# Matmuls that only keep TensorE running, an opening in another order, and keys and values projected two batches ahead, in a decoder layer on one core

## What is computed

```
x = x + self_attention(layernorm(x))          # 2 heads of 64, rotary, causal
x = x + cross_attention(layernorm(x), ctx)    # 16 heads of 8, 1601 keys
x = x + ffn(layernorm(x))                     # 512 hidden, exact gelu, weights changed per batch

Q = split_heads(query @ Wq + bq); K = split_heads(ctx @ Wk + bk); V = split_heads(ctx @ Wv + bv)
attn = softmax(einsum("bhqd,bhkd->bhqk", Q, K) / sqrt(8)); out = attn @ V @ Wo + bo
```

## Time and profile before

| | |
|---|---|
| three timed runs | 414.47, 417.73, 417.07 us; median 417.07 |
| the profiled execution | 413.62 us |
| its span | 411.8 us |
| busy, share of the span | TensorE 87%, VectorE 74%, ScalarE 73%, GpSimd 32% |
| mean granted TensorE clock | 0.925 |
| first maximum, first score | 39.3 us, 60.2 us |
| end of unit 0, of batch 0, 1, 2, 3 | 90.8, 150.0, 236.7, 323.2, 391.9 us |

### The profile page before, as it was taken

How to read it: one execution, slowest core, us unless ns; L and a number is a source line. 1 busy time by engine, 2 the same in 40 slices (tenths; PEclk the granted TensorE clock), 3 DMA queues, 4 the chain that set the end, 5 groups by cost and what they waited for, 6 DMA issues and landing times.

```text
span 411.8 us, 11548 instructions
## 1 busy us (share of the span) xinstructions
PE 357.9 (87%) x4598; PEld 164.8 (40%) x4598; DVE 306.6 (74%) x692; ACT 299.4 (73%) x637; POOL 131.6 (32%) x205
## 2 busy tenths in 40 slices
PE   1645988989989989999898999998989999798946
PEld 0332333444534444444344444444334344353334
DVE  2373998779889988798788887998778899690022
ACT  1321226888979799889697898897697998969921
POOL 5721000379120206897200137992000036000010
PEclk9966555999999999999999999999899999999968
DMA  7063370003507312235160331343211420000000
GB/s 294 12 240 122 139 249 40 2 27 130 173 27 169 123 38 60 93 130 163 35 173 14 107 96 53 121 136 96 80 40 47 130 61 21 2 15 2 2 0 15
DMA packets 22203, 35.77 MB, mean 87 GB/s; under 512 B 1604, under 2 KB 19694, under 8 KB 22150
## 3 DMA queue, kind: packets, MB, share of 16 engines
q1 hardware_dynamic: 22150, 35.05, 26.8%
HBM read 19.25 MB, written 11.96 MB: 76 GB/s over the span
## 4 chain that ended last, share of the span: by engine, by line
PE 47%; DMA 13%; POOL 12%; ACT 11%; DVE 7%; issue 5%; SPq 4%; POOLq 0%; ACTq 0%; DVEq 0%
PE wsum L1013 16%; PE score L1027 10%; PE ring L983 8%; PE ring L1047 8%; DMA q_rows<-q_parts 5%; ACT probs L873 5%; POOL k_parts L547 4%; DMA k_rows<-k_parts 4%; POOL k_rest L584 3%; POOL k_parts L589 3%; DVE part_max L690 2%; DMA k_unit<-k_rows 2%; DMA q_unit<-consts 1%; SPq L435 1%; POOL xn L600 1%
## 5 line engine op out<-in xcount | busy, mean ns | idle before, releaser
L690 DVE TENSOR_REDUCE part_max<-ring 128x1 f32<-128x401 f32 x512 | 261.0, 568 | 43.8 <-PE ring L1047 42.8
L873 ACT ACTIVATE probs<-score 128x512 f32<-128x512 f32 (+1 forms) x416 | 223.1, 597 | 41.6 <-PE score L1027 38.1
L1047 PE MATMUL ring<-k_unit,q_unit 51*128 51x401 bf16 x512 | 143.2, 355 | 9.9 <-DMA q_unit<-consts 5.1
L1013 PE MATMUL wsum<-probs,v_unit 128*32 128x256 f32 (+1 forms) x1664 | 135.7, 394 | 2.0 <-ACT unit_ctx L878 2.0
L1027 PE MATMUL score<-q_unit,k_unit 51*128 51x256 bf16 (+1 forms) x832 | 123.9, 278 | 7.3 <-ACT probs L873 5.0
L1027 PEld LDWEIGHTS score<-q_unit,k_unit 51*128 51x128 bf16 (+1 forms) x832 | 47.2, 97 | 100.6 <-ACT probs L873 60.9
L1047 PEld LDWEIGHTS ring<-k_unit,q_unit 51*128 51x128 bf16 x512 | 47.3, 95 | 30.1 <-DVE part_max L690 10.8
L1013 PEld LDWEIGHTS wsum<-probs,v_unit 128*32 128x32 f32 (+1 forms) x1664 | 39.7, 109 | 41.3 <-issue 24.6
L547 POOL TENSOR_TENSOR max_parts<-neg_max,c_sb 128x8 bf16<-128x8 f32 x16 | 3.4, 210 | 150.8 <-DVE neg_max L694 150.7
L621 POOL TENSOR_SCALAR prob_norm<-prob_self,prob_rsum 128x128 f32<-128x128 f32 (+1 forms) x12 | 9.0, 766 | 43.1 <-DVE prob_rsum L766 43.1
L927 ACT ACTIVATE v_aug<-ring 128x128 f32<-128x128 f32 (+1 forms) x60 | 10.5, 261 | 16.1 <-PE ring L983 16.1
(11 more groups left out here) (111 smaller groups left out, 290.3 us busy)
## 6 DMA issues: line engine op xcount, KB each, us to landing
k_unit<-k_rows SPq DMA_DIRECT2D x32, 300.2 KB
v_unit<-v_aug SPq DMA_DIRECT2D x16, 234.0 KB, 5.9
ctx_sb<-ctx_t SPq DMA_DIRECT2D x4, 800.5 KB, 7.4
k_rows<-k_parts SPq DMA_DIRECT2D x4, 601.5 KB, 3.2
k_rows<-k_parts SPq DMA_DIRECT2D x4, 599.2 KB, 3.4
k_rows<-k_parts SPq DMA_DIRECT2D x4, 401.0 KB, 4.1
k_rows<-k_parts SPq DMA_DIRECT2D x4, 399.5 KB, 4.1
even<-ffn_rows SPq DMA_DIRECT2D x3, 512.0 KB, 3.8
```

The costliest lines, as they stand in the source:

```text
L690: v_.tensor_reduce(part_max[:, par, q, head, hp, c:c + 1], ring[s][:, 0:CW], AX.X, ALU.max)\
L873: a_.activation(probs[0:rows, i % PB, :], score[i % EB][0:rows, :], ACT.Exp)\
L1013: last = mm(wsum[32 * j:32 * j + 32, 0:S], v_unit[0:rows, u, VQ * t + VW * j:VQ * t + VW * j + 32], probs[0:rows, i % PB, S * (j // 2):S * ...
L1047: mm(ring[s][:, 0:CW], q_unit[rows, u, hp, P * q:P * (q + 1)], k_unit[rows, u, L * hp + (CW - 1) * c:L * hp + (CW - 1) * c + CW], start=Tr ...
```

## The change

Four things are changed together.

1. **Kept matmuls.** `keep(n)` issues n matmuls of a zero tile, 128 by 128 by 512, bf16, into the first bank of scores. 20 stand at the very start, before TensorE waits for weights; 21 in six other places up to unit 0; 13 in two places at the end.
2. **The opening's order.** `U0` to `U6` and the load of values move ahead of unit 0's maxima. Batch 1's keys and values (`K0` to `K3`, `V0` to `V3`) and their stores stand between these maxima. Batch 0's qk_rot goes from GpSimd to VectorE. Of batch 0's keys the 32 rows of unit 0 are stored first, with a semaphore of their own; their load follows at once, and then come the other 96 rows. GpSimd's adds x1_bo and x2_b2 wait in batch 0 and at the end until VectorE has made the normalised tile.
3. **Two batches ahead.** In `SIDE` the items of keys and values name batch b+2 instead of b+1, so batch 2 has none. ctx_sb and v_aug are there twice.
4. **The queue.** The key load of a later batch's first unit moves from `store1` to `split`, behind the store of queries.

```diff
 SIDE = {
-    (3, 0): [("ctx", 2)],
+    (3, 0): [("ctx", 3)],
...
-    (1, 8): [("prep", "q", 1), ("prep", "store1", 1)], (1, 9): [("prep", "split", 1)],
+    (1, 8): [("prep", "q", 1), ("prep", "store1", 2)], (1, 9): [("prep", "split", 1)],
...
-FIRST = [("ln1", 0), ("ln1", 1), ("xT", 0), ("qk", 0), ("qks", 0), ("K0", 0), ("K1", 0), ("e0", 0), ("e1", 0), ("soft", 0),
...
+FIRST = [("keep", 20), ("ln1", 0), ("ln1", 1), ("xT", 0), ("qk", 0), ("qks", 0), ("K0", 0), ("K1", 0), ("keep", 5),
+         ("e0", 0), ("e1", 0), ("soft", 0), ("pn", 0), ("K2", 0), ("K3", 0), ("store0", 0), ("v", 0), ("xT", 1), ("keep", 6),
+         ("qk", 1), ("pT0", 0), ("pT1", 0), ("av", 0), ("store1", 0), ("wo", 0), ("U0", 0), ("U1", 0), ("U2", 0), ("U3", 0),
+         ("keep", 3), ("ln2", 0), ("x2T", 0), ("q", 0), ("split", 0), ("qks", 1), ("keep", 3), ("pick", 0),
+         ("U4", 0), ("U5", 0), ("U6", 0), ("load", 0), ("keep", 2)]
+
+BETWEEN = (("K0",), ("K1",), ("K2",), ("K3", "store0"), ("V0",), ("V1",), ("V2",), ("V3", "store1"))
+POST_LAST = ["OT", "Wo", "keep", "ln3", "x3T", "low0", "low1", "h0", "h1", "keep", "out"]
+KEEP_LAST = (10, 3)
...
-    for i in range(7):
-        plan += [("M", 0, k) for k in range(4 * i, 4 * i + 4)] + [("prep", f"U{i}", 0)]
...
+    for i in range(MU // 4):
+        plan += [("M", 0, k) for k in range(4 * i, 4 * i + 4)] + [("prep", name, 1) for name in BETWEEN[i]]
+    plan += [("ctx", 2)]
+    return plan + [("M", 1, k) for k in range(4)] + [("keep", 2), ("mT", 0)] + [("M", 1, k) for k in range(4, AHEAD_FIRST)]
...
+                        first = 0 if b else D // UB
+                        for t0, t1 in RUNS if first else ():
+                            sp.dma_start(k_rows[b, t0:t1, 0:first, keys].rearrange("t r n -> r t n"),
+                                         k_parts[0:first, 0:t1 - t0, keys]).then_inc(first_keys_written, 16)
+                        if first and h == 1:
+                            load_keys(b, 0)
                         for t0, t1 in RUNS:
-                            sp.dma_start(k_rows[b, t0:t1, :, keys].rearrange("t r n -> r t n"),
-                                         k_parts[:, 0:t1 - t0, keys]).then_inc(keys_written, 16)
-                        if h == 1:
-                            load_keys(b, 0)
+                            sp.dma_start(k_rows[b, t0:t1, first:D, keys].rearrange("t r n -> r t n"),
+                                         k_parts[first:D, 0:t1 - t0, keys]).then_inc(keys_written, 16)
...
                         if b:
+                            load_keys(b, 0)
                             load_queries(b, 0)
...
+                        if b == 1:
+                            pool.wait_ge(first_keys_written, 32 * len(RUNS))
+                        if b:
+                            pool.wait_ge(keys_written, 32 * len(RUNS) * b)
...
+                        else:
+                            pool.wait_ge(xn2_done, 1)
...
+                    else:
+                        pool.wait_ge(xn3_done, B)
...
+                    if nb == 0:
+                        wait_drained(("prep", "qk", nb))
+                        wait_drained(item)
+                        v_.tensor_tensor(qk_rot[:, :], rope_a[:, :], rope_b[:, :], ALU.add).then_inc(qk_done, 1)
...
+                    if nb:
+                        act.wait_ge(k_split[c // 2], 4 * nb)
...
+            def keep(n):
+
+                for _ in range(n):
+                    mm(score[0][:, :], still[:, 0:P], still[:, :], start=True, stop=True)
```

More of the change, by code:

```diff
@@ L148 @@
 }
-FIRST = [("ln1", 0), ("ln1", 1), ("xT", 0), ("qk", 0), ("qks", 0), ("K0", 0), ("K1", 0), ("e0", 0), ("e1", 0), ("soft", 0),
-         ("pn", 0), ("K2", 0), ("K3", 0), ("store0", 0), ("v", 0), ("xT", 1), ("qk", 1), ("pT0", 0), ("pT1", 0), ("av", 0),
-         ("store1", 0), ("wo", 0), ("ln2", 0), ("x2T", 0), ("q", 0), ("split", 0), ("qks", 1), ("pick", 0)]
-POST_LAST = ["OT", "Wo", "ln3", "x3T", "low0", "low1", "h0", "h1", "out"]
+FIRST = [("keep", 20), ("ln1", 0), ("ln1", 1), ("xT", 0), ("qk", 0), ("qks", 0), ("K0", 0), ("K1", 0), ("keep", 5),
[6 more added lines that the diff above has]
+KEEP_LAST = (10, 3)
 AHEAD = (14, 13, 7, 10)
@@ L665, in _ @@
             v_ = nc.vector
+            v_.memset(still[:, :], 0.0).then_inc(still_set, 1)
             dve.wait_ge(x_in, 16)
@@ L1131, in prep @@
                     at = CW * int(name[1])
-                    strips(ring[s][:, 0:CW], W("Wk"), ctx_sb[:, at:at + CW]).then_inc(filled[s], 1)
+                    strips(ring[s][:, 0:CW], W("Wk"), ctx_sb[:, nb % 2, at:at + CW]).then_inc(filled[s], 1)
                 elif name == "pick":
```

72 lines of the change are left out of this document (42 added, 30 removed).

## The result

| | before | changed |
|---|---|---|
| median, same chip | 415.8 us (414.3 to 417.7) | 399.6 us (398.1 to 402.6) |
| ratio | | 0.962, 95% interval 0.954 to 0.969 |
| profiled execution | 413.6 us, span 411.8 | 398.1 us, span 396.2 |

The change makes the kernel 3.8% faster. Every ratio here is taken over the executions within 1.5% of the fastest of the same kernel; the medians are over all of them. The forecast was 392.5 us in a range of 386 to 402: the direction holds and the time lies in the range, 7 us above the point. It lies outside the 387 to 397 that the forecast gave its own case. Profile against profile the gain is 15.5 us where the sum said 22.3.

A forecast was written before the change was run, and what follows sets the result against it. TensorE was taken to bound the steady part, latency and the low clock the opening, small steps at low clock the end. Terms summed to -22.3 from 413.6, 391.3; a third of 3.4 added gave 392.5 us, range 386 to 402.

The forecast's parts named there:

- its own case: Whole kernel: the changes act as its terms say, time within 387 to 397 us; chance 0.64.
- the sum: Whole kernel: all terms from first score to end added, -22.3 us on the profiled 413.6, so 391.3.
- First 20 kept matmuls, faster first projections: Start: kept matmuls end near 7.5 us without delay; projections at full clock bring first energies at 13.4, 1.7 us earlier.
- Keys of unit 0: Opening: storing 32 rows first lands in 2.3 us, load issued at 27.9, first maximum at 36.2, -3.0 us.
- Strips between the maxima: Opening: eight rounds at VectorE's pace take 16.2 us for 17.3, -1.1; GpSimd's queue adds 0.7, the turn gives 0.3.
- The 1.3 for two rounds at the low clock: First maxima: TensorE idles some 2.5 us before them, so 1.3 us was added for two rounds at the low clock.
- Unit 0 at the full clock, -4.9: First unit after the first score: steps of 1.24 us at full clock, 8.6 us for 13.7; bounds 0 and 5.1.
- the three signs: Wrong if clock reads 0.50 in 45 to 70 us, first maximum stays at 39, or third batch stays above 82.
- Waits for queries, -5.0 and -1.6: Steady part: TensorE's three waits for q_unit, 5.1 us, vanish, and the half clock behind the third with them.
- Third batch, -5.5: Third batch: without keys and values it issues 7.46 us fewer TensorE records, ending at 77 us; bounds 0 and 7.5.
- End, -2.9: End of the kernel: kept matmuls hold the full clock and GpSimd's add waits; output at 407.0, 2.9 us sooner.
- the rival of a low clock: Opening: clock stays low through maxima and unit 0, maxima 21.9 us for 17.5, no 4.9 gain, 402 us; chance 0.15.

The follow-up runs named there:

- Experiment 6: The changed kernel with all 128 rows of the first batch's keys stored before unit 0's load, instead of 32 rows first; median 407.7 us.
- experiment 10: The changed kernel run once more, unedited; median 400.2 us, ratio 0.959, its profiled execution 405.2 us.
- experiment 8: The changed kernel with more kept matmuls, the second batch's first key strips ahead of the first maximum, and matmuls of zeros in unit 0 and Gelu passages; median 398.2 us.
- experiment 9: The changed kernel with the third batch's context load earlier, 398.2 us; also with a key strip earlier, kept matmuls and matmuls of zeros, 393.8 us; a third kernel followed.
- experiment 5: The changed kernel with keys and values projected one batch ahead and none between the first maxima; median 400.1 us, ratio 0.963.
- experiment 4: The changed kernel with 25 zero-adding matmuls of 256 columns in the last batch's Gelu passage; median 399.3 us.
- Experiment 2: The kernel before the change with only the kept matmuls added, at the nearest places; median 415.8 us, ratio 0.992.
- Experiment 1: The changed kernel with every kept matmul left out; median 405.7 us.
- 7: The changed kernel with the second batch's first two key strips ahead of the first maximum, replacing two kept matmuls, other strips spread over eight rounds; median 398.2 us.
- the last of 9: The 393.8 us kernel (early context load, key strip ahead, kept matmuls and matmuls of zeros) with 14 more kept matmuls in the opening; median 398.4 us.

## Why the prediction was right and wrong, step by step

- *First 20 kept matmuls, faster first projections.* Right: they ended at 7.4 (7.5 forecast), energies at 13.3 (13.4), VectorE's key split at 23.7 (24.0). Their records lie 0.43 us apart to 4.9 us, so the first ones ran at 1.2 GHz, as the durations of the earlier trace rows had said, while the granted clock reads 1.00. From 4.9 us they lie 0.22 apart, with nothing but matmuls of zeros run until then. The five kept ones in front of the energies ended at 13.37, no more than 0.2 us behind qk_rot.
- *Keys of unit 0.* Right in kind, 1.0 short: the store landed in 2.18 (2.3), the load was issued at 27.0 (27.9), since the last issue came 1.1 us behind the split and not 1.6. Experiment 6 agrees with the store's 2.0, though the store landed late in two of eleven profiles. In the second profile of the same program queries and not keys set the first maximum (experiment 10), which the forecast had ruled out with a `pick` that ends near 32.6: it ended at 35.7 there, behind a low clock from 22.9 to 29.7.
- *Strips between the maxima.* Rounds of 2.0 with keys as forecast, 2.27 with values (ScalarE drains a group of values in four pieces and the ring waits for it), together 16.8 for 16.2. From the maxima's end to the first score 4.0 us passed for 3.3, a loss of 0.7 where queue and turn had been put at 0.4. **The 1.3 for two rounds at the low clock did not come**: the clock held through the maxima. Hence -4.2 for -2.4; with the first profile's luck of no fall near 23 us taken away it was -2.0 (experiment 10).
- *Unit 0 at the full clock, -4.9.* **This step failed, on three counts.** The clock fell at 56.0, behind 4 us in which TensorE waited for the last maxima, GpSimd's queue and the turn. The forecast had looked for a fall at the first maximum and not for what the faster rounds leave starved at their end. Second, had it held, the context's load was next in line (experiment 8); the sentence on what is late next went only to the queries. Third, its size was wrong: with both cured the gain was 2.9 us, and by the busy shares VectorE and ScalarE set the pace (experiment 9). Of the three signs that the forecast gave for being wrong one came in half: the clock read 0.50 from 56 to 69.6.
- *Waits for queries, -5.0 and -1.6.* Right: no maximum waits for q_unit in the changed kernel's first profile, and one for 0.5 us in its second. It is the queries' place in SP's order that did it (experiment 5). The two waits in batches 0 and 1 were 2.9 us, and these batches gained 3.0.
- *Third batch, -5.5.* Right in kind, mis-sized: 4.0 for 5.5 (experiment 5). Of the 7.5 us of records TensorE's busy time gave back 4.8, and its idle time rose from 4.1 to 4.9 (82.36 less 78.26, 78.32 less 73.47). VectorE, busy for 90% of the batch, did not take over by this share.
- *Batch 3.* Not in the sum: +2.9. No edit touches it; the clock fell at 342.7 behind the Gelu passage. The kernel before has the same passage, and its clock held in its one profile; without added matmuls the clock fell there in five of ten profiles, whatever the opening (experiment 4), so an even chance of +2.9 was missing from the sum. ScalarE's rows there, in order of time, are two table loads around the Gelu, 1.28 us each. From 335.7 to 339.9 it makes no exponentials, for which TensorE waits:

```profile
335.70 1.28 ACT L997 ACT_TABLE_LOAD   x1
...
336.99 1.57 ACT L997 ACTIVATE hidden<-ring,w_sb 128x256 f32<-128x256 f32 x4
...
338.58 1.28 ACT L909 ACT_TABLE_LOAD   x1
```

The Trainium skill (ScalarE: Activation LUTs, "What ACT_TABLE_LOAD costs") gives some 1283 ns for such a load; the trace agrees.
- *End, -2.9.* Right: -3.0. Experiment 2, the old end with kept matmuls, has 17.4 us for 19.9 with the clock at 1.00, so 2.5 of it are theirs, and the rest of the change gives 0.5. Experiment 1 takes them out of the new end and loses 1.2 only; the clock was low there for 6.8 us and not for the 10.3 of the kernel before. The kept ones do not always hold it: in four profiles with them (experiments 4, 5, 7 and the last of 9) it fell for 3.4 us, and the end took 17.4 to 17.5.
- *The total.* The sum was 6.8 us too deep in the profiled execution. Unit 0 (4.8), batch 3 (2.9) and the three batches (0.9) fell short, the opening gave 1.8 more. The measured time lies in the stated range because that reached to 402 for the rival of a low clock. Of maxima and unit 0 the clock was low in unit 0 alone, so the rival came true for one half, and the opening's surplus covered part of what batch 3 lost: that is luck.

The rival of a clock that stays low was priced nearly right (maxima of 21.9 forecast, 22.9 in experiment 1). It came where the kept ones are missing, and also with all of them behind a wait of 3.3 us for the keys (experiment 5).

## What to carry to other kernels

A stretch in which TensorE waits in small pieces can cost its clock for the next 3 to 17 us here, and in some executions only: one profile cannot price such a place, so look for starved stretches, not for falls, and count the falls over all profiles that have the place unedited. Filling them pays where TensorE truly waits and the clock often falls (here in a Gelu passage, at 0.4 to 0.9 us each time for 2.9 in half of the profiles) and costs where its work and another engine's already add up to the round. When a stretch is to get faster, ask for every load what its slack is at the new pace: the low clock had hidden a late one.

## What the runs showed of the hardware

The clock can fall without any long pause. In the two stretches shown of the changed kernel no wait of TensorE was longer than 1.4 us, its busy share was 34 to 70%, and the clock halved. It fell behind single pauses as well: 3.3 us in experiment 5, 3.5 in experiment 2. The Trainium skill (TensorE: Matmul & The Clock Gate, "A second HAM failure mode: psum-queue depth-cycling") describes such pauses between groups of matmuls, frequent enough for the clock to swing; the traces agree, and add that the same stretch of one program falls in one execution and not in the next (the third batch's: at 296 us in the second profile, not at all in the first). Matmuls on zeros are enough to bring the clock up: in the changed kernel the first 20, with nothing ahead of them, lie 0.43 us apart to 4.9 us and 0.22 from there. By the counts they help to hold it: no fall in ten Gelu passages that had them, nine in 32 that had not (experiment 4). They can go into an accumulator that is open anyway, where they add nothing.
